# One product of e and V per key tile, placed between the two pairs of transposed scores

## The reference

```python
Q, K, V = ...                          # linear and conv projections of x
scores = einsum('bhqd,bhkd->bhqk', Q, K) / sqrt(16)
scores = scores * tau[..., None] + delta[:, :, None, :]
out = einsum('bhqk,bhkd->bhqd', softmax(scores), V)
x = layernorm(x + linear(out))
x = layernorm(x + fp4_block_quantised_linear(x) + bias)
```

## Time and profile before

| | us |
|---|---|
| median of 3 runs | 1715.76 |
| lowest and highest run | 1709.59, 1721.31 |
| the profiled execution, its own time | 1709.64 |
| its span, first to last instruction | 1707.8 |
| PE busy | 1639.0 (96%) |
| DVE busy | 1536.4 (90%) |
| ACT busy | 1325.2 (78%) |

### The profile page before, as it was taken

The page is one execution under the profiler, slowest core; times in us unless marked ns, Lnnn a source line. Parts: engine busy times, 40 slices in busy tenths (PEclk is TensorE's granted clock), DMA queues, the critical chain, the costliest instruction groups (busy, mean ns, idle before and its releaser), DMA issues.

```text
span 1707.8 us, 33648 instructions
## 1 busy us (share of the span) xinstructions
PE 1639.0 (96%) x13978; PEld 742.4 (43%) x13978; DVE 1536.4 (90%) x1622; ACT 1325.2 (78%) x2401; POOL 74.5 (4%) x133
## 2 busy tenths in 40 slices
PE   8999989999999999999999999999999999999775
PEld 7677754333333333333333333333333333334564
DVE  5688978999999999999999999999999999973896
ACT  3788724888888888888888888888888888886333
POOL 3000002000000000000000000000000000010110
PEclk9999999999999999999999999999999999999988
DMA  3377336000600060023004100602060000002331
GB/s 110 99 183 185 106 95 91 8 8 8 83 8 9 13 78 12 10 35 57 8 8 61 34 8 8 85 9 82 8 84 8 8 8 15 8 10 55 104 123 50
DMA packets 46960, 84.72 MB, mean 50 GB/s; under 512 B 9116, under 2 KB 21020, under 8 KB 44092
## 3 DMA queue, kind: packets, MB, share of 16 engines
q1 hardware_dynamic: 44952, 82.49, 22.6%
q10 hardware_dynamic: 1856, 0.09, 0.1%
HBM read 51.36 MB, written 30.67 MB: 48 GB/s over the span
## 4 chain that ended last, share of the span: by engine, by line
PE 61%; DVE 22%; ACT 2%; issue 1%; ACTq 0%; POOL 0%; DVEq 0%
PE ps L826 26%; PE ps L813 20%; DVE mx L215 17%; PE ps L205 11%; PE ps L885 1%; DVE work L1052 1%; ACT y L944 1%; PE ps L901 1%; ACT o_sb L944 1%; DVE small L1047 0%; PE ps L800 0%; PE ps L891 0%; DVE stats L1026 0%; PE ps L857 0%; DVE work L1061 0%
## 5 line engine op out<-in xcount | busy, mean ns | idle before, releaser
L215 DVE TENSOR_REDUCE mx<-ps 128x2 f32<-128x1024 f32 x1024 | 1233.0, 1223 | 58.8 <-PE ps L205 49.2
L967 ACT ACTIVATE e<-ps 128x512 f32<-128x512 f32 x2048 | 1110.1, 596 | 198.7 <-PE ps L813 158.5
L826 PE MATMUL ps<-e,v_grp 128*32 128x256 f32 x8192 | 655.1, 392 | 0.5 <-ACT ev L956 0.5
L813 PE MATMUL ps<-q,k 52*128 52x512 f32 x2048 | 523.8, 497 | 3.8 <-ACT e L967 3.8
L205 PE MATMUL ps<-k,q 50*128 50x512 f32 x2048 | 420.0, 402 | 10.9 <-DVE mx L215 6.2
L813 PEld LDWEIGHTS ps<-q,k 52*128 52x128 f32 x2048 | 198.9, 183 | 429.0 <-ACT e L967 399.6
L826 PEld LDWEIGHTS ps<-e,v_grp 128*32 128x32 f32 x8192 | 161.5, 108 | 358.6 <-issue 199.4
L205 PEld LDWEIGHTS ps<-k,q 50*128 50x128 f32 x2048 | 198.0, 187 | 39.1 <-DVE mx L215 30.4
L605 PE MATMUL ps<-x_p,m_p 128*128 128x512 f32 x576 | 141.3, 401 | 0.0
L605 PEld LDWEIGHTS ps<-x_p,m_p 128*128 128x128 f32 x576 | 107.7, 190 | 30.6 <-issue 5.7
L437 DVE SCALAR_TENSOR_TENSOR hid<-x_c,dw_w,hid 128x512 f32<-128x512 f32 x128 | 88.5, 747 | 13.2 <-ACT hid L379 13.2
(11 more groups left out here) (117 smaller groups left out, 658.2 us busy)
## 6 DMA issues: line engine op xcount, KB each, us to landing
k<-k_parts SPq DMA_DIRECT2D x42, 256.0 KB
q<-q_parts SPq DMA_DIRECT2D x42, 256.0 KB
k_parts<-k_sp SPq DMA_DIRECT2D x16, 512.0 KB, 4.9
q_parts<-q_sp SPq DMA_DIRECT2D x16, 512.0 KB, 4.5
att<-ev SPq DMA_DIRECT2D x32, 256.0 KB
x_c<-in_x_t SPq DMA_DIRECT2D x8, 514.0 KB, 6.4
tau_r<-tau_rows SPq DMA_DIRECT2D x16, 256.0 KB
x_in<-in_x SPq DMA_DIRECT2D x8, 512.0 KB, 3.7
```

What stands on the lines that cost most here:

```text
L215: nc.vector.tensor_reduce(mx[:, j % 2, :, jh, qt, kc], ps[:, b0:b0 + 2, :], AX.X, ALU.max).then_inc(s_free, 1)
L813: nc.tensor.matmul(ps[:, st_bank(n), :], k_set[r, g % 2, jh, kt * P:(kt + 1) * P], q_set[r, g % 2, jh, lo:lo + CH], start=True, stop=True) ...
L826: last = nc.tensor.matmul(ps[32 * h:32 * (h + 1), 0, PVW * part:PVW * (part + 1)], v_grp[:, kt, h, :], e[:, x % E_BUFS, h * CH + PVW * par ...
L967: nc.scalar.activation(e[:, x % E_BUFS, h * CH:(h + 1) * CH], ps[:, st_bank(n), :], ACT.Exp).then_inc(e_ready, 1)
```

## The change

TensorE's order within a key tile changes. Before, it was product (256 queries), pair 0, one item of the maximum, product (256 queries), pair 1, one item of the maximum. After, it is pair 0, product (512 queries), pair 1, two items of the maximum. The product is one call of four heads over all 512 queries. The number of scores, exponentials and reductions stays, as do the buffers and what each step waits for. The 33rd item of an iteration falls, as before, behind the last step of the iteration, which now means three items in a row there.

```diff
-            PVW = CH // 2
...
-                    def pv_half(i, kt, part):
+                    def pv(i, kt):
 
                         x = KT * i + kt
-                        if part == 0:
-                            if kt == 0 and i > 0:
-                                pe.wait_ge(att_evac, i)
-                            if i % NQ == 0 and kt % 4 == 0:
-                                pe.wait_ge(v_ready, 4 * (i // NQ) + kt // 4 + 1)
-                            pe.wait_ge(e_ready, HG * (x + 1))
+                        if kt == 0 and i > 0:
+                            pe.wait_ge(att_evac, i)
+                        if i % NQ == 0 and kt % 4 == 0:
+                            pe.wait_ge(v_ready, 4 * (i // NQ) + kt // 4 + 1)
+                        pe.wait_ge(e_ready, HG * (x + 1))
                         for h in range(HG):
-                            last = nc.tensor.matmul(ps[32 * h:32 * (h + 1), 0, PVW * part:PVW * (part + 1)], v_grp[:, kt, h, :],
-                                                    e[:, x % E_BUFS, h * CH + PVW * part:h * CH + PVW * (part + 1)],
-                                                    start=(kt == 0 and part == 0), stop=(kt == KT - 1 and part == 1), skip_group_check=True)
-                        if part == 1:
-                            last.then_inc(pv_done, 1)
+                            last = nc.tensor.matmul(ps[32 * h:32 * (h + 1), 0, :], v_grp[:, kt, h, :], e[:, x % E_BUFS, h * CH:(h + 1) * CH],
+                                                    start=(kt == 0), stop=(kt == KT - 1), skip_group_check=True)
+                        last.then_inc(pv_done, 1)
...
-                            for jh in range(HH):
-                                pv_half(i, k, jh)
-                                if x + AHEAD < NIT * KT:
-                                    st(x + AHEAD, jh)
-                                while issued < first + min(due, due * (2 * k + jh + 1) // slots):
-                                    s_item(issued)
-                                    issued += 1
+                            if x + AHEAD < NIT * KT:
+                                st(x + AHEAD, 0)
+                            pv(i, k)
+                            if x + AHEAD < NIT * KT:
+                                st(x + AHEAD, 1)
+                            while issued < first + min(due, due * (2 * k + 2) // slots):
+                                s_item(issued)
+                                issued += 1
```

## The result

| | before | after |
|---|---|---|
| median, us | 1716.09 (4 runs) | 1798.76 (4 runs) |
| lowest to highest | 1709.59 to 1721.31 | 1798.48 to 1803.01 |
| ratio, 95% interval | 1 | 1.0499 [1.0469, 1.0529] |
| span of the profiled execution | 1707.8 | 1796.9 |

The change costs 5.0%; the forecast was 1786 us, in a range of 1752 to 1808.

The account below looks back on a forecast made before the run. Today TensorE's chain and the wait through ScalarE's exponential both give 1.24 us per half step. Iterations 0 to 29 +73 us, iteration 30 +2.9, iteration 31 +1.8 and -3, together +74: 1786 us median, range 1752 to 1808.

Parts of the forecast that it names:

- The ring: Each key tile: pair 0's second matmul waits for pair 1's first exponential, 1.18 us; tile 2.60 us instead of 2.48.
- The third item: End of each iteration: the last of three maximum items waits for a reduction's banks, 1.1 us once per iteration.
- The rule on the array's shape: TensorE drains when tiling mode changes, about 0.11 us each; two changes per tile instead of four, the saving lying before a wait.
- 0.22 us from item to item: Behind pair 1: two maximum items in a row need no change of shape, so they start 0.22 us apart.
- The DMAs behind the rows: Pair 0 of tile 14 could start 4.2 us behind the rows' copy; loss between nothing and 1.0 us per iteration, nothing taken.
- The sum: Whole kernel: all terms together +74 us on the profiled execution's 1709.6 us, giving 1784, and 1786 us for the median.
- the 0.05 us for the copy of the finished product: Each iteration: copying the finished product waits for a product that ends later, costing 0.05 us.
- 12 tiles x 0.12 and 4 without items: Iteration 30: twelve tiles 0.12 us longer, four without maximum items going from 2.24 to 2.60; +2.9 us.
- (1): Faster: TensorE's own work is the bound, the exponential's wait doesn't bind; tile 2.43 us, 1690 us; 6 in 100.
- (2): No change: waiting matmul's weights loaded ahead and passes at their low bound, tile 2.46 us, about 1720 us; 7 in 100.
- (3): Small loss: only weights loaded ahead or only cheaper passes, tile 2.51 to 2.55 us, 1740 to 1762 us; 7 in 100.
- (4): Slower still: the rows land late, at up to 1.0 us per iteration, +30, 1815 us; 7 in 100.

Follow-up runs that it names:

- experiment 1: Exponentials done for 256 of 512 queries from the fifth key tile on: 1718.4 us in the changed kernel, 1705.1 us in the kernel before.
- experiment 2: Changed kernel with one of the two maximum items moved between the product and pair 1: 1900.7 us, ratio 1.1077.
- experiment 4: Kernel before with one part of the change: whole product at the tile's head, 1942.6 us; or both items behind pair 1, product in halves, 1941.2 us.
- experiment 6: Changed kernel with ten pairs of idle matmuls in front of TensorE's last wait for the maximum, in iteration 30: 1792.3 us, ratio 1.0449.
- experiment 3: Changed kernel, order kept, with the product as two calls of 256 queries one behind the other: 1795.5 us, ratio 1.0468.
- experiment 5: Third item moved to the tile with the rows: 1775.5 us in the changed kernel, 1844.2 us in the kernel with halved product and both items behind pair 1.

## Why the prediction was right, step by step

**The ring, right.** "The first exponential of a pair must have ended before the second matmul of the next pair" is what the trace of the changed kernel shows, and what experiment 1 takes away. The tile was forecast at 2.60 us and is 2.60 to 2.61; the same sum gave 2.82, 2.91, 2.70 and 2.43 for the four variants in experiments 1, 2 and 4, and 2.84, 2.91, 2.71 and 2.42 were measured. Its terms hold one by one: 1.19 (1.18) from pair 1 to the second matmul, 0.42 to the product, 0.99 (1.00) to pair 1.

**The third item, right.** 1.1 us forecast, 1.12 measured. Beside it one reading was off: two reductions in a row were taken as 1.22 us from start to start, against the 1.13 worked out in the same paragraph. The second was to end 3.23 us behind pair 1; it ended 3.13 behind it (902.79 + 2.36, from 902.02). It was hidden either way.

**The rule on the array's shape, as weighed.** The rows fit it, and what the new order saves is spent in front of the wait. No row that the prediction names shows its 0.22 us from item to item; in experiment 2 an item starts 0.23 us behind pair 1 (902.48 to 902.71), so that a change of shape costs about 0.10 us in front of a product (0.33 less 0.23). With the exponentials out of the way (experiment 1) the new order's tile is 2.42 us against the old one's 2.48. That is what the rule could promise here, and it still was no gain: the third item takes it back, iterations are 40.2 us in both orders, and the new one is at 1718.4 us against 1705.1.

**The DMAs behind the rows, right.** Pair 0 of tile 14 starts 4.21 us behind the copy of the rows, where 4.2 was forecast, and no tile of an ordinary iteration is longer than 2.61 us but the last. So the first scores of the next iteration never waited for the DMAs. Nothing beyond the trace tested it.

**The sum, 13 to 15 us short.** 74 us were forecast between the profiled executions and 89 came. Iterations 0 to 29: 73 forecast, 75.8 measured. Tiles of 2.61 us and not 2.60 add nearly 5; the 0.05 us for the copy of the finished product, 1.5 in all, did not come. The largest part is iteration 30, forecast at +2.9 and measured at +9.5: the term that failed is "12 tiles x 0.12 and 4 without items". Its tiles were priced at the full clock and the wait for the last maximum wasn't looked at. The last scores and the last transposition now fall into one step of TensorE's order, and the wait between them grew from 1.22 to 2.23 us; the clock fell behind it. With the wait filled (experiment 6) the fall is gone and 6 us with it. But the kernel of experiment 3 waits as well and kept its clock, and two kernels whose last wait was only 1.22 and 1.23 us lost it. So the wait goes ahead of the fall and doesn't always bring it, and the longer wait isn't shown to be the reason; what decides was not settled. In iteration 31, 1.2 us were to be gained and 1.9 were lost: most tiles with a projection came to 3.36 us, within the 3.3 to 3.4 forecast, but the first two tiles still run at half the clock, 4.07 and 4.36 us instead of 2.23 and 2.83. The 1.9 us on both sides of the loop were not traced further.

**The rivals.** None came. (1) would have needed the second matmul not to wait; (2) and (3) needed cheaper passes or weights loaded ahead, and the terms came out at the values taken; (4) needed late DMAs.

## What to carry to other kernels

When two engines hand a few buffers back and forth, write down for each hand-over the least distance between two uses, and lay the other work so that it fills these distances evenly. Here two rings of 1.24 and 1.18 us want 2.42 us of other work, in two equal portions; the old order gave 1.24 and 1.24, the new one 1.42 and 0.78, and the short one is filled up with waiting while the long one is paid in full. Less work in a badly divided order is slower than more work in a well divided one, and a page that says "TensorE 94%" shows nothing of it.

## What the runs showed of the hardware

- *A wait can cost more behind it than in it.* Behind TensorE's idle wait of 2.23 us the granted clock was 0.5 (1.2 GHz) for 27 us, with tiles of 4.07 us instead of 2.61. Behind waits of 1.09 us once in an iteration it fell in 18 places of one execution, and the times spread from 1911 to 1967 us; with the item elsewhere one fall was left, behind a wait of 0.80 us. Waits of 0.99 us once in an iteration, in the changed kernel, were followed by no fall. That the wait matters is shown by taking it away (experiments 5 and 6); neither that it suffices nor that its length decides is.
- *Passes of 256 and of 512 columns stream alike* in a run of products: 1.07 us for sixteen records or for eight.
- *A matmul whose weights come late holds up the one behind it too.* Where an item's weights are loaded ahead, the product starts 0.33 us behind it; where weights and matmul start at the same moment, behind a wait, the product comes 0.42 us (903.21 to 903.63) and 0.44 us later (883.39 to 883.83).
